# An FFN kernel for one core: loads, convolution and weight preparation of its first phase in another order

## The reference

```python
def _L0_cond_ref(x, c, weight, c_weight, bias):      # 4 groups, 9 taps
    out = lax.conv_general_dilated(x, weight, window_strides=(STRIDE,), padding=[(PAD, PAD)], ...)
    ctx = jnp.einsum('nd,od->no', c, c_weight)
    return out + ctx[:, :, None] + bias[None, :, None]
...
def _L0_ffn_ref(input_act, weight):                  # 8-bit weights and rows
    w_scale = jnp.max(jnp.abs(weight), axis=-1, keepdims=True) / QMAX
    w_q = jnp.round(weight / w_scale).astype(jnp.int8)
    a_scale = jnp.max(jnp.abs(input_act), axis=-1, keepdims=True) / QMAX
    x_q = jnp.round(input_act / a_scale).astype(jnp.int8)
    acc = jnp.matmul(x_q.astype(jnp.int32), w_q.T.astype(jnp.int32))
    out = (acc.astype(jnp.float32) * (a_scale * w_scale.T[None, :, :])).astype(jnp.float16)
...
def _L1_cond_ref(...):                               # channels mixed by weights that depend on the batch
    h = gelu(embedding @ W0 + b0); h = gelu(h @ W1 + b1)
    att = softmax(h @ W2 + b2)
    agg_w = jnp.einsum('bk,koi->boi', att, weight[..., 0]); agg_b = att @ bias_k
    out = jnp.einsum('boi,bih->boh', agg_w, x) + agg_b[:, :, None]
...
    w = kernel.astype(x.dtype) * 2.0 - 1.0           # _L1_ffn_ref: signs
    return scale * jnp.einsum('bsi,if->bsf', x, w)
...
    x = x + _L0_ffn_ref(_L0_cond_ref(...)); x = x + _L1_ffn_ref(_L1_cond_ref(x, ...))
```

## Time and profile before

| | |
|---|---|
| median of 3 runs | 134.8 us (134.45 to 135.58) |
| profiled execution, its own time | 136.74 us |
| its span | 135.0 us |
| busy: PE, DVE, POOL, ACT | 118.2, 73.1, 64.9, 45.7 us |
| granted PE clock, mean | 0.885 |

### The profile page before, as it was taken

How to read it: one execution, slowest core, us unless ns; L and a number is a source line. 1 busy time by engine, 2 the same in 40 slices (tenths; PEclk the granted TensorE clock), 3 DMA queues, 4 the chain that set the end, 5 groups by cost and what they waited for, 6 DMA issues and landing times.

```text
span 135.0 us, 4401 instructions
## 1 busy us (share of the span) xinstructions
PE 118.2 (88%) x1811; PEld 84.2 (62%) x1811; DVE 73.1 (54%) x176; ACT 45.7 (34%) x91; POOL 64.9 (48%) x89
## 2 busy tenths in 40 slices
PE   5959749999439979998999999999999999799970
PEld 5745327967217746775676866777687776587840
DVE  2535705720562139904992983687399298756422
ACT  0404107198430164046408303431630632330200
POOL 7920430730065406760676387078447718856430
PEclk9975555557975799999999999999999999999999
DMA  1999999999403800074556876585250422222222
GB/s 22 222 207 310 203 239 223 223 217 241 83 0 117 194 12 0 35 198 83 169 166 202 231 182 199 121 243 147 80 160 0 160 93 63 78 79 81 78 78 78
DMA packets 11778, 18.60 MB, mean 138 GB/s; under 512 B 2184, under 2 KB 3048, under 8 KB 11760
## 3 DMA queue, kind: packets, MB, share of 16 engines
q1 hardware_dynamic: 10736, 18.10, 52.3%
q10 hardware_dynamic: 864, 0.20, 0.9%
q0 software_dynamic: 160, 0.04, 0.4%
HBM read 14.12 MB, written 4.19 MB: 136 GB/s over the span
## 4 chain that ended last, share of the span: by engine, by line
PE 73%; DVE 8%; issue 7%; DMA 5%; ACT 2%; SPq 2%; DVEq 0%; ACTq 0%
PE ps L309 26%; PE ps L354 11%; PE ps L357 10%; PE ps L346 9%; PE ps L339 9%; DMA xs<-in_x_dram 5%; PE ps L288 3%; PE ps L331 2%; DVE res L565 2%; DVE delta L550 2%; PE ps L267 1%; SPq L199 1%; DVE c_scale L534 1%; ACT xq L665 1%; ACT ysb L659 1%
## 5 line engine op out<-in xcount | busy, mean ns | idle before, releaser
L309 PE MATMUL ps<-xs,conv_st 32*32 32x256 f32 x1280 | 35.1, 462 | 3.0 <-issue 2.8
L765 POOL TENSOR_TENSOR x<-xr,delta 128x512 f32<-128x512 f32 x16 | 18.6, 1166 | 32.0 <-DVE delta L550 32.0
L309 PEld LDWEIGHTS ps<-xs,conv_st 32*32 32x32 f32 x1280 | 21.3, 113 | 12.8 <-issue 7.1
L757 POOL TENSOR_SCALAR rounded<-ysb,c_inv 128x256 f32<-128x256 f32 x32 | 14.7, 478 | 19.2 <-DVE c_inv L536 19.2
L520 DVE TENSOR_REDUCE row_max<-ysb 128x2 f32<-128x512 f32 x16 | 10.9, 683 | 22.9 <-ACT ysb L659 22.9
L671 ACT ACTIVATE z_hi<-z 128x512 fp32r<-128x512 f32 x16 | 10.1, 631 | 37.5 <-DVE z L558 37.5
L771 POOL TENSOR_TENSOR z_lo<-z,z_hi 128x512 fp32r<-128x512 f32 x16 | 20.4, 1276 | 4.5 <-ACT z_hi L671 3.4
L354 PE MATMUL ps<-sign,z_hi 128*128 128x512 f32 x64 | 18.8, 415 | 1.8 <-DVE res L565 1.7
L339 PE MATMUL ps<-wq,xq 128*128 128x512 f16 x64 | 17.4, 396 | 3.1 <-ACT xq L665 1.9
L346 PEld LDWEIGHTS ps<-mix,x 128*128 128x128 f32 x128 | 17.7, 200 | 2.5 <-issue 0.4
L346 PE MATMUL ps<-mix,x 128*128 128x128 f32 x128 | 17.7, 284 | 0.0
(11 more groups left out here) (98 smaller groups left out, 86.7 us busy)
## 6 DMA issues: line engine op xcount, KB each, us to landing
xs<-in_x_dram SPq DMA_DIRECT2D x32, 256.0 KB, 5.7
xr<-in_x_dram SPq DMA_DIRECT2D x16, 256.0 KB, 4.2
out_dram<-res SPq DMA_DIRECT2D x16, 256.0 KB, 2.0
q_raw<-in_L_ffn_weight_dram SPq DMA_DIRECT2D x4, 256.0 KB, 7.5
sign_raw<-in_L_ffn_kernel_dram SPq DMA_DIRECT2D x1, 256.0 KB, 11.4
w_sb<-in_L_cond_W_dram ACTq DMA_DIRECT2D x2, 64.0 KB, 5.5
cond_raw<-in_cond_dram ACTq DMA_DIRECT2D x1, 32.0 KB, 2.1
b_col<-in_L_cond_b_dram ACTq DMA_DIRECT2D x2, 0.5 KB, 6.0
```

The costliest lines, as they stand in the source:

```text
L309: mm = pe.matmul(Y[r][C * j:C * (j + 1), HL * qs[0]:HL * (qs[-1] + 1)], conv_st[C * r:C * (r + 1), m].rearrange("k o p -> k (o p)"), xs[C ...
L757: last = nc.gpsimd.tensor_scalar(rounded[:, t % 4, g, :], ysb[:, t % 4, g, :], c_inv[:, q, h, g:g + 1], ROUND, ALU.mult, ALU.add)
L765: nc.gpsimd.tensor_tensor(x1[:, t % NX1, :], xr[:, t % 4, :], delta[:, t % 2, :], ALU.add)\
```

## The change

Nothing of the result changes. Loads: SP issues x of tile 0, 2 and 3 first, ACT the weights of the convolution and x of tile 1 ahead of its small inputs; the quantised weights come behind x of tile 3, and SP now waits for landings of earlier transfers between its issues. PE: the convolution of tiles 0 and 1 is cut into its five steps with hidden1, the bias products and hidden2 between them; that of tiles 2 and 3 follows at once, ahead of all `ffn0_weights`. `fold` products are 10 and not 20, bias products 4 and not 16. Dummy products are float16 of 512 columns. The copies of the mixing weights are spread: POOL takes 8 from an SBUF copy (agg_sb), ACT and DVE 4 each. The DMAs of aggb_row move from ACT to POOL, ahead of the signs. The diff, cut to its core:

```diff
-    WARM = (7, 3)
+    WARM = (9, 3, 4)
...
+            def load_x(t, s):
                 need(sp, conv_done, t // 2 - 2 * NX + 1)
-                q, h = t // 2 % 2, t % 2
-                for s in range(SH):
-                    sp.dma_start(xs[64 * h + s:64 * (h + 1):SH, slot(t), q, :, PAD - s:PAD - s + L],
-                                 x[NB * t:NB * (t + 1)].rearrange("b c l -> c b l")).then_inc(x_in[slot(t)][q], 16)
+                load_shift(sp, t, s)
...
-            sp.wait_ge(pad_zeroed, 1)
-            sp.dma_start(conv_pad[:, :, 1:1 + TAPS], conv_w).then_inc(conv_in, 16)
             sp.wait_ge(pads_set, 2)
-            load_x(0)
-            load_x(1)
-            for a in range(LC):
+            load_x(0, 0)
+            load_x(0, 1)
+            def load_q(a):
                 sp.dma_start(q_raw[:, a, :], ffn0_w[P * a:P * (a + 1), :]).then_inc(q_in[a], 16)
-            load_x(2)
-            load_x(3)
+            load_x(2, 0)
+            sp.wait_ge(x_in[0][0][0], 32)
+            load_x(2, 1)
+            sp.wait_ge(x_in[0][0][1], 32)
+            load_x(3, 0)
+            load_x(3, 1)
+            sp.wait_ge(x_in[0][1][0], 32)
+            load_q(0)
+            load_q(1)
+            sp.wait_ge(x_in[0][1][1], 32)
+            load_q(2)
+            load_q(3)
+            sp.wait_ge(q_in[1], 16)
             load_rows(0)
+            sp.wait_ge(q_in[2], 16)
             sp.dma_start(sign_raw[:], ffn1_w.rearrange("(a p) f -> p a f", p=P)).then_inc(sign_in, 16)
+            sp.wait_ge(q_in[3], 16)
             load_rows(1)
-            load_x(4)
-            load_x(5)
-            load_x(6)
-            load_x(7)
+            sp.dma_start(scale_col[:], ffn1_scale.partition_broadcast(P)).then_inc(scale_in, 16)
+            sp.wait_ge(xr_in[0], 16)
+            load_x(4, 0)
+            sp.wait_ge(sign_in, 16)
+            load_x(4, 1)
+            sp.wait_ge(xr_in[1], 16)
+            load_x(5, 0)
+            load_x(5, 1)
+            sp.wait_ge(x_in[1][0][0], 32)
             load_rows(2)
             load_rows(3)
-            sp.dma_start(scale_col[:], ffn1_scale.partition_broadcast(P)).then_inc(scale_in, 16)
+            sp.wait_ge(x_in[1][0][1], 32)
+            load_x(6, 0)
+            sp.wait_ge(xr_in[2], 16)
+            load_x(6, 1)
+            sp.wait_ge(xr_in[3], 16)
+            load_x(7, 0)
+            load_x(7, 1)
             for t in range(4, NT + 5):
                 if t + 4 < NT:
-                    load_x(t + 4)
+                    load_x(t + 4, 0)
+                    load_x(t + 4, 1)
...
-            warm(WARM[0])
+            warm(WARM[0], ACC)
...
+            warm(WARM[1], ACC)
+            pe.wait_ge(conv_copied, 2)
+            conv_inputs(0, [0])
+            conv_step(0, [0], 0)
+            pe.wait_ge(cond_copied, 3)
             hidden1()
-            pe.wait_ge(fside_copied, 1)
+            conv_step(0, [0], 1)
+            pe.wait_ge(fside_copied, 2)
             for g in range(2):
-                for j in range(NB):
-                    pe.matmul(FIN[C * j:C * (j + 1), 256 + NT * g:256 + NT * (g + 1)],
-                              cond_wT[:, CH * g:CH * (g + 1)].rearrange("d o p -> d (o p)"),
-                              cond_T[:, j:B:NB], start=True, stop=False, tile_position=(0, C * j))
-                for j in range(NB):
-                    mm = pe.matmul(FIN[C * j:C * (j + 1), 256 + NT * g:256 + NT * (g + 1)],
-                                   fside_rep[:, CH * g:CH * (g + 1)].rearrange("a o p -> a (o p)"),
-                                   ones[0:1, 0:NT], start=False, stop=True, tile_position=(0, C * j))
+                at = 256 + B * g
+                pe.matmul(FIN[:, at:at + B],
+                          cond_wT[:, g].rearrange("d j o p -> d (j o p)"),
+                          cond_T[:], start=True, stop=False)
+                mm = pe.matmul(FIN[:, at:at + B],
+                               fside_rep[:, g].rearrange("a j o p -> a (j o p)"),
+                               ones[0:1, 0:B], start=False, stop=True)
             mm.then_inc(ctx_ready, 1)
+            conv_step(0, [0], 2)
+            conv_step(0, [0], 3)
             hidden2()
-            conv_inputs(0, [0])
-            pe.wait_ge(conv_copied, 1)
-            for m in range(MS):
-                mm = conv_step(0, [0], m)
-                if m == 1:
-                    logits()
-            mm.then_inc(conv_done, 1)
+            conv_step(0, [0], 4).then_inc(conv_done, 1)
+            pe.wait_ge(ident_h_ready, 2)
+            pe.wait_ge(bias_copied, 1)
+            logits()
+            warm(WARM[2], IDLE)
+            conv_inputs(0, [1])
+            conv_step(0, [1], 0)
+            conv_step(0, [1], 1)
+            conv_step(0, [1], 2)
             attention()
-            pe.wait_ge(ident_h_ready, 2)
+            conv_step(0, [1], 3)
+            conv_step(0, [1], 4).then_inc(conv_done, 1)
             ffn0_weights(0)
             ffn0_weights(1)
-            pe.wait_ge(bias_copied, 1)
             mixing_weights()
             ffn0_weights(2)
             ffn0_weights(3)
...
-            conv(0, [1])
+            pe.wait_ge(y_ready, 8)
             ffn0_scales()
+            pe.wait_ge(wq_ready, LC)
+            turn_tile(0)
             pe.wait_ge(wsc_ready, 1)
-            turn_tile(0)
             ffn0_tile(0)
             turn_tile(1)
-            spread_bias(0, 1)
             ffn0_tile(1)
             pe.wait_ge(agg_copied, 2)
+            pe.wait_ge(agg_spread, 2 * NB)
+            spread_bias(0, 1)
             mix_tile(0)
...
-            ffn0_maximum(0)
-            ffn0_maximum(1)
-            ffn0_inverses(0)
-            softmax_first()
-            ffn0_maximum(2)
-            softmax_second()
-            ffn0_maximum(3)
-            ffn0_inverses(1)
-            attention_copy()
             dve.wait_ge(rowm_ready, 1)
             dve.tensor_reduce(low_high[:], row_mask[:].rearrange("r (k h) -> r h k", h=2), AX_X, ALU.add)\
                .then_inc(low_high_ready, 1)
             dve.wait_ge(low_high_ready, 1)
+            softmax_first()
             maxima(0)
+            softmax_second()
             maxima(1)
+            ffn0_maximum(0)
+            ffn0_maximum(1)
+            ffn0_inverses(0)
+            attention_copy()
             scales(0, 2)
+            ffn0_maximum(2)
+            ffn0_maximum(3)
+            ffn0_inverses(1)
...
+            act.dma_start(conv_raw[:], conv_w).then_inc(conv_in, 16)
+            act.wait_ge(pads_set, 2)
+            load_shift(act, 1, 0)
+            load_shift(act, 1, 1)
...
-                for ol in range(OL - 1):
-                    for b in range(NB):
-                        last = act.activation(mix_block(b, ol), agg_block(b, ol), ACT.Copy)
+                act.activation(agg_sb[0:2 * C], FIN[0:2 * C], ACT.Copy).then_inc(agg_in, 1)
+                for b in range(NB):
+                    last = act.activation(mix_block(b, OL - 2), agg_block(b, OL - 2), ACT.Copy)
                 last.then_inc(agg_copied, 1)
...
-            exponentials()
             convolved(0, 0)
             convolved(0, 1)
+            exponentials()
             convolved(1, 0)
             convolved(1, 1)
+            convolved(2, 0)
+            convolved(2, 1)
             ffn0_weights(0)
             ffn0_weights(1)
+            convolved(3, 0)
+            convolved(3, 1)
             ffn0_weights(2)
             ffn0_weights(3)
             mixing_weights()
-            act.wait_ge(aggb_lo, 1)
-            for h in range(2):
-                act.dma_start(aggb_row[h:h + 1, :].bitcast(F32).rearrange("a (b o) -> a b o", b=B),
-                              aggb[:, h, :].bitcast(F32)).then_inc(aggb_rows, 16)
-            convolved(2, 0)
-            convolved(2, 1)
             quantised(0)
...
+            def round_weights(h):
+                pool.wait_ge(q_inverted, h + 1)
+                for a in (2 * h, 2 * h + 1):
+                    nc.gpsimd.tensor_scalar(q_round[:, a, :], q_raw[:, a, :], q_inv[:, a:a + 1], ROUND, ALU.mult, ALU.add)\
+                      .then_inc(q_rounded, 1)
...
+            round_weights(0)
             quantise(0)
             quantise(1)
+            round_weights(1)
+            pool.wait_ge(mix_zeroed, 1)
+            pool.wait_ge(agg_in, 1)
+            pool.wait_ge(quant_done, 2)
+            for ol in range(OL - 2):
+                for b in range(NB):
+                    need(pool, agg_spread, NB * ol + b)
+                    nc.gpsimd.tensor_copy(mix_block(b, ol), agg_block(b, ol, agg_sb)).then_inc(agg_spread, 1)
+            pool.wait_ge(agg_spread, 2 * NB)
+            pool.wait_ge(aggb_lo, 1)
+            for h in range(2):
+                pool.dma_start(aggb_row[h:h + 1, :].bitcast(F32).rearrange("a (b o) -> a b o", b=B),
+                               aggb[:, h, :].bitcast(F32)).then_inc(aggb_rows, 16)
             pool.wait_ge(sign_in, 16)
```

104 lines of the change are left out of this document (60 added, 44 removed).

## The result

The changed kernel takes 143.32 us, the median of 4 runs (141.05 to 144.22), where the kernel before took 135.19 beside it (134.45 to 135.97): a ratio of 1.0509, interval 1.0337 to 1.0681. It is slower, by more than the range allowed. Executions that came out over 1.5% above the fastest of their kernel, here 143.54 and 144.22, are left out of every ratio with an interval, and four profiles further down (e2, e3, e9, e15, marked d in the table) are of such executions, so that their clock and lengths are rough.

The account below looks back on a forecast made before the run. PE bounds the loop, so its arrival at the loop's first convolution counts. Of 2.9 us won at the front, the exponential takes 1.8 and POOL's list the rest: net -0.3, median 134.5 us, range 131.4 to 137.8.

Parts of the forecast that it names:

- The sum: Path to the loop's first convolution: start at 43.4 against 43.73, net -0.3, median 134.5 give or take 1.5; chance 0.47.
- cond_w in, PE starts: Front, ACT's queue: cond_w lands between 8.8 and 10.1, taken as 9.5, when PE starts.
- small products between them: Between the first convolution's steps: 14 records at 0.04 to 0.23 each, 0.5 to 3.2 us, taken as 1.4.
- POOL's list: From agg_sb to x1 of tile 0: copies 3.0, DMA issues 1.1, signs, quantise and first_sum; 9.0 us, with gaps ready at 41.5.
- 2.9 us won at the front: First convolution's end: 18.1 against 20.98 before, a gain of 2.9, as much as the hole.
- The steps of the convolution cover them: First convolution: w0 and b0 wanted some 3 us later, w1 8 us later, so the steps cover their landing.
- The table load: Between ACT's copies, in the wait for y_ready: load 1.28 plus exponential some 0.5; wait 3.4, without the skill's drain.
- The clock: Mixing weights behind the second convolution: full clock, about 2 us; at 0.50, 4.0 and ACT's copy ends at 33.9.
- The faster front: Rival: cond lands with x at 8.8, first convolution takes 3.5 instead of 5.8; total 131.5; chance 0.24.
- The hole comes back elsewhere: Rival: PE runs out of instructions in the second convolution, which stops before its end; price 2.8, total 137.3; chance 0.21.
- against it: Argument against the returning hole: SP's waits keep fewer transfers outstanding; no size given.
- the loop is PE's, and the change leaves its orders alone: Loop from its first convolution at 43.73 on: length unchanged, each microsecond ahead of it is one at the end.

Follow-up runs that it names:

- e2: Changed kernel with all twelve mixing copies and the two aggb_row DMA issues back on ACT; 143.31 us over 135.48 for the kernel before.
- e3: Changed kernel with steps 0 and 1 of the first convolution ahead of the products that need cond and cond_w; ratio 1.0319 to the kernel before.
- e9: e5 with SP's waits only as far as x of tile 3, none behind it; ratio 0.9879 to the kernel before.
- e15: e11 with cond, cond_w and w0 ahead of x of tile 1 on ACT's queue; ratio 1.0138 to the kernel before.
- e6: Changed kernel with the bias products narrow as before, 16 instead of 4 wide ones; 144.44 us, one execution.
- e1: Changed kernel with POOL's signs ahead of its mixing copies, before the wait for agg_sb; ratio 1.0457 to the kernel before.
- e7: Changed kernel with a dummy exponential behind the second GELU, loading the table ahead of ACT's first copy; 143.04 us, one execution.
- e13: Changed kernel with the attention chain and mixing weights placed as in the kernel before, POOL's copies between its roundings; ratio 1.0512 to the kernel before.
- e14: e13 plus narrow bias products and one step of the first convolution ahead of cond; ratio 1.0288 to the kernel before.
- e4: Changed kernel without SP's waits for landings between x of tile 2 and x of tile 7, same order; ratio 1.1120 to the kernel before.
- e11: Kernel before with the changed kernel's transfers (SP list with waits, convolution weights and x of tile 1 from ACT), old engine lists; ratio 0.9893.
- e5: Kernel before with SP waits keeping about four large transfers under way, x of tiles 6 and 7 later; 129.70 us, ratio 0.9626.
- e8: Changed kernel with the edits of e1, e3, e6 and e7 together; 137.30 us over 135.14 for the kernel before.
- e12: Kernel before with one dummy product instead of seven at its start, 12 PE records fewer; 137.5 us, one execution.

## Why the prediction was wrong

The sum ended at 43.4 for the loop's first convolution; it was 48.5. By its own steps:

| step | forecast | measured | off |
|---|---|---|---|
| cond_w in, PE starts | 9.5 | 10.9 | +1.4 |
| dummies | 1.4 | 1.4 | 0 |
| steps of the first convolution | 5.8 | 5.7 | -0.1 |
| small products between them | 1.4 | 4.3 | +2.9 |
| wait for y_ready, with the table load | 3.4 | 3.4 | 0 |
| second convolution | 5.8 | 5.8 | 0 |
| its end to agg_sb ready | 5.0 | 4.8 | -0.2 |
| agg_sb to x1 of tile 0, POOL's list | 9.2 | 10.1 | +0.9 |
| mix_tile | 1.9 | 2.1 | +0.2 |

**The step that failed** is "Between them stand 14 records of small products ... I take 1.4, nearer the short ones because most have few columns". A float32 product of 128x64 takes 0.62 at the half clock (two records of 0.31), and there are six of them; with the transposes and what lies around them 4.3. The upper bound per record, 0.23 from the mixing weights with their 8 rows, was itself too low. So of "2.9 us won at the front" nothing came: the first convolution ended at 22.3, 1.3 later than ACT began to empty it before. e6 shows that the wide form costs 1.6 of this.

**The start** was the second error. Both ends that I gave for cond_w (8.8 and 10.1) were below the 10.7 at which it landed: 48 KB stood behind two transfers of 256 KB on one queue. "The steps of the convolution cover them" I said of w0, b0 and w1 only, and for these it held: PE waits for none of them. cond_w is asked for ahead of the steps, where nothing covers it. e3 turned that round and gained 3.1 at this place.

**POOL's list** was right in kind: it was busy to first_sum(0) with 0.4 us of gaps beyond those between the copies, and released the last link, as e1 shows. The copies took 0.41 each with 0.05 between them, 3.9 to the first DMA issue, instead of 3.0. The DMA of aggb_row landed in 1.8 and cost nothing.

**The table load** held. Its wait came out at 3.4. The next activation starts at 24.46, 0.01 behind the load's end, and the load 0.02 behind the copy ahead of it. The Trainium skill ("ScalarE: Activation LUTs", what ACT_TABLE_LOAD costs) gives a drain of 1380 ns besides; this trace, as the one of before, shows none on either side. e7 shows what the load costs on the path: the wait is 0.95 shorter without it.

**The clock** came out as taken: 1.00 through the mixing weights, 1.99. That was near an edge, since other fronts (e6, e13 and e14) left them at 3.0 to 3.67.

**The rivals.** The faster front did not come: cond was late, and the first convolution ran at 1.09 for 32 records, at a granted clock of 0.50. "The hole comes back elsewhere" happened in the changed kernel only as the pause of 0.41, but the reading behind it was right, and it was right about the place: without SP's waits it comes in the second convolution (e4). What I put "against it", that SP's waits keep fewer transfers outstanding, was the strongest effect of the whole change, and I gave it no price. The Trainium skill ("Runtime: NRT & Kernel Launch", instruction fetch mechanics) holds such fetches to be mostly hidden; here holes of up to 4.19 us were the cost when SP's queue was deep, and of 0.71 at most when it was not.

**What I did not see** is the loss behind the second convolution, against the kernel before. The sum held nearly all of it, 16.1 of 17.0 us, so it is no large part of the miss; but I compared sums of the new path with the old mark, not stretch with stretch, and so let the 5.2 that this stage costs over the kernel before eat up what the front was to gain. The lists moved the mixing weights, the quantised weights and their turning from PE's wait for ACT, which dummies then filled, to behind the second convolution. That is 10.9 us become 17.0. e11 bounds it from the other side: same transfers, old lists, and the loop starts at 40.0.

**The loop** was 1.4 longer than before, against "the loop is PE's, and the change leaves its orders alone". Its first convolution ends with a stop of 0.28, another of 0.44 comes later, both of the kind that the trace puts down to nothing; which other share is the clock isn't settled. The miss is 8.8 us (134.5 against 143.3): 5.1 by the table, 1.4 in the loop, and 1.9 from the shift from profile to median that I took over, the rest small: the profiled execution of before was 1.9 above its median, that of the changed kernel at its median.

**What stays open:** which of SP's waits do the work in e5, and whether its waits with x of tile 1 from ACT would gain more; neither was tried. Nor is it shown why the executions of e8 scatter by 2.3% and those of e9 by 5.4%, where those of e5 scatter by 1.3%, or how long the hole of e9 is in its other executions. And since there is one profile of before, 1.9 above its median, each "earlier than before" here may be up to 1.9 too large.

## What to carry to other kernels

An in-order engine that stops for nothing the profile shows may be out of instructions: see whether the stop moves by the count of instructions that you take away ahead of it, and whether a packet of instructions ends just ahead of the restart, and then limit how many large transfers are under way, with waits on landings in the queue that issues them; that was worth 3.7% on the untouched lists. Move small products out of an engine's wait for another one only if something of use takes their place, and price them at their own width and clock. When a change has two halves (transfers and lists), price each by itself: here the transfers gained 1% on the old lists, and the new lists lost 6% with the new transfers.

## What the runs showed of the hardware

- A stop of PE follows the count of its instructions: 12 records fewer ahead of it, and it came 12 records later (e12); 24 more, and it came 24 records earlier (e8 against e4). Nine holes stood behind 220, 345 to 347 or 598 records, and each ended 1.3 to 1.7 us after a 16 KB packet on the queue named instruction.
- With SP's queue unlimited a 256 KB transfer took 12.9 us from issue to landing, with waits 5.0 (e5); the mean over 3 to 40 us was 198 and 187 GB/s. Small transfers behind it paid too: aggb_row, 8 KB, 9.73 us in e9 and 1.8 in the changed kernel; cond, 32 KB, 7.2 behind two transfers of 256 KB on its own queue, 2.1 without them.
- POOL needs 0.41 us for a float32 copy of 32x128, more than the 0.30 of its 128x128 cast, which has four times the rows.
- Work that PE does earlier is not won where its clock then falls: e6 had the first convolution 1.9 earlier, then 3.67 for the mixing weights instead of 1.99, and its loop started 1.3 later (one execution).
